# Moving a 2 KB load, six small operations and two weight loads in an attention and feed-forward kernel

## The reference

```python
def _rfs(xw, ab, AB, gs):
    dot_products = jnp.einsum('...d,rd->...r', xw, ab[:, None] * gs)
    correction = (0.5 * jnp.sum(xw * xw, axis=-1))[..., None] * (ab * ab)
    return 1.0 / math.sqrt(NUM_RFS) * AB * jnp.exp(dot_products - correction)
# ab = xis, AB = exp(xis)
weights = _rfs(input_weights, ab, AB, proj_matrix)
feats = _rfs(x, ab, AB, proj_matrix)
attn = einsum('bsr,or->bso', feats, weights)
x = layernorm(x + attn)
h = silu(x @ w_gate.T / 127) * (x @ w_up.T / 127)      # 3072 wide, int8 weights
x = layernorm(x + h @ w_down.T / 127)
```

## Time and profile before

| | |
|---|---|
| median of 3 runs | 740.23 us (739.68 to 740.56) |
| the profiled execution, its own time | 739.75 us |
| its span (slowest core, core 6) | 738.2 us |
| spans of the 8 cores | 735.7 to 738.2 us |
| TensorE matmul busy | 697.6 us, 95% |
| ScalarE busy | 197.1 us, 27% |
| VectorE busy | 183.9 us, 25% |
| mean granted TensorE clock, by core | 0.988 to 0.991 |

### The profile page before, as it was taken

The page is one execution under the profiler, slowest core; times in us unless marked ns, Lnnn a source line. Parts: engine busy times, 40 slices in busy tenths (PEclk is TensorE's granted clock), DMA queues, the critical chain, the costliest instruction groups (busy, mean ns, idle before and its releaser), DMA issues.

```text
span 738.2 us, 8975 instructions; the slowest of 8 cores (735.7 to 738.2 us)
## 1 busy us (share of the span) xinstructions
PE 697.6 (95%) x3357; PEld 314.1 (43%) x3424; DVE 183.9 (25%) x329; ACT 197.1 (27%) x322; POOL 9.1 (1%) x21
## 2 busy tenths in 40 slices
PE   2999999999959999999999999999999999999994
PEld 0333435343424444444444444444444444444442
DVE  1120335262532211121221122221222131211222
ACT  1223335252522111043311104231110523111122
POOL 2000000000000000000000000000000000000000
PEclk9999999999979999999999999999999999999998
DMA  8991030871084000001200000120000100000011
GB/s 120 168 353 44 1 57 1 211 303 57 2 334 179 0 1 1 1 28 58 87 0 1 1 1 29 58 86 1 0 1 1 57 29 29 0 1 2 1 58 57
DMA packets 5835, 44.63 MB, mean 60 GB/s; under 512 B 800, under 2 KB 800, under 8 KB 3104
## 3 DMA queue, kind: packets, MB, share of 16 engines
q0 software_dynamic: 2192, 27.27, 13.5%
q1 hardware_dynamic: 3600, 16.78, 6.0%
HBM read 30.42 MB, written 12.58 MB: 58 GB/s over the span
## 4 chain that ended last, share of the span: by engine, by line
PE 86%; DMA 7%; DVE 3%; issue 2%; ACT 1%; POOL 0%; DVEq 0%; ACTq 0%; SPq 0%; POOLq 0%
PE pt L624 23%; PE P L586 22%; PE P L682 22%; PE P L429 5%; DMA bfarena<-iwT 4%; PE P L276 4%; PE P L323 4%; DMA bfarena<-xfm 2%; PE pt L462 1%; PE P L688 1%; PE P L698 1%; PE P L435 1%; PE P L441 1%; PE P L281 1%; DVE bfarena L367 1%
## 5 line engine op out<-in xcount | busy, mean ns | idle before, releaser
L586 PE MATMUL P<-bfarena 128*128 128x512 bf16 x752 | 183.9, 383 | 0.9
L624 PE MATMUL pt<-bfarena 128*128 128x512 bf16 x753 | 180.3, 379 | 0.9
L682 PE MATMUL P<-bfarena 128*128 128x512 bf16 x721 | 162.2, 379 | 0.9
L637 DVE SCALAR_TENSOR_TENSOR bfarena<-pt,bfarena 128x512 bf16<-128x512 f32 x96 | 66.4, 692 | 245.2 <-PE pt L624 239.3
L605 ACT ACTIVATE bfarena<-P 128x512 bf16<-128x512 f32 x96 | 57.3, 597 | 239.6 <-PE P L586 235.6
L586 PEld LDWEIGHTS P<-bfarena 128*128 128x128 bf16 x768 | 75.4, 99 | 93.4 <-issue 3.5
L624 PEld LDWEIGHTS pt<-bfarena 128*128 128x128 bf16 x768 | 74.9, 98 | 92.4
L682 PEld LDWEIGHTS P<-bfarena 128*128 128x128 bf16 x736 | 71.9, 98 | 88.7
L367 DVE TENSOR_SCALAR_CACHE_REDUCE bfarena<-P 128x1024 bf16<-128x1024 f32 x32 | 39.2, 1225 | 199.0 <-PE P L698 145.3
L276 PE MATMUL P<-bfarena 128*128 128x512 bf16 x249 | 62.2, 388 | 2.8 <-DMA bfarena<-projT 2.5
L387 ACT ACTIVATE f32arena<-f32arena 128x1 f32<-128x1 f32 x32 | 9.4, 295 | 174.8 <-DVE f32arena L384 173.9
(11 more groups left out here) (54 smaller groups left out, 234.8 us busy)
## 6 DMA issues: line engine op xcount, KB each, us to landing
out<-f32arena SPq DMA_DIRECT2D x16, 512.0 KB, 2.7
bfarena<-wgT POOLq DMA_DIRECT2D x1, 6144.0 KB, 53.2
bfarena<-wdT POOLq DMA_DIRECT2D x3, 2048.0 KB, 14.7
bfarena<-wuT POOLq DMA_DIRECT2D x1, 4608.0 KB, 27.4
x1s<-bfarena SPq DMA_DIRECT2D x4, 1024.0 KB, 4.5
bfarena<-x1s SPq DMA_DIRECT2D x4, 1024.0 KB, 6.3
bfarena<-xfm POOLq DMA_DIRECT2D x3, 1024.0 KB, 15.1
bfarena<-projT POOLq DMA_DIRECT2D x2, 1024.0 KB, 18.6
```

Of the source, the lines that this page charges most:

```text
L586: return e.matmul(pg, bf(WGT_O + dk * 3072 + hc * 128, 128), bf(xb1 + dk * 512, 512), start=(dk == 0), stop=(dk == DK - 1))
L624: return e.matmul(puj, bf(wu_off + hc * 128, 128), bf(xb1 + dk * 512, 512), start=(dk == 0), stop=(dk == DK - 1))
L637: "vector", "VE", lambda e, j=j, hc=hc, puj=puj: e.scalar_tensor_tensor(hact_ap(hc, 0, 512), puj, 1.0 / 16129.0, sg_ap(j), OP.mult, OP.mult))
L682: e.matmul(P1[:, base + oh * 512:base + oh * 512 + 512], hact_ap(hc, m * 128, 128), bf(reg + (hc % 8) * 1024 + oh * 512, 512), start=(hc = ...
```

## The change

Four edits. (1) The load of xisr is issued after the two halves of the projection matrix instead of before them. (2) VectorE's six constant operations are emitted after the first tile's two squares instead of before them. (3) Of the three loads of wdT only the first is issued at the end of the first stage; the second is issued once gate block 2 is done and the third once gate block 4 is done. (4) The silu results go through two buffers instead of three, so silu j waits for product j-2.

```diff
@@ the arena's offsets
-SG3_O = WUT1_O + 18432
-BF_END = SG3_O + 512
+BF_END = WUT1_O + 18432
@@ the first loads
-        ev["ld_abrow"] = dma("gpsimd", "Lab", bfr(ABROW_O, 1024), xisr_h[:, :])
         ev["ld_projT"] = dma("gpsimd", "Lpj", bf(PROJT_O, 4096), projT_h[:, 0:4096])
         ev["ld_projT2"] = dma("gpsimd", "Lpj2", bf(PROJT_O + 4096, 4096),
                               projT_h[:, 4096:8192])
+        ev["ld_abrow"] = dma("gpsimd", "Lab", bfr(ABROW_O, 1024), xisr_h[:, :])
@@ the constants: these lines stood ahead of emit_ones_mm's definition
         emit_xsq(0)
+        ftmp = fa(FTMP_O, DK)
+        em.wait("vector", "XR", XR_ALL)
+        em.inc("vector", "VE", lambda e: e.memset(ones_col, 1.0))
+        em.inc("vector", "VE", lambda e: e.memset(epsc, 1e-5))
+        em.inc("vector", "VE", lambda e: e.memset(c512, 512.0))
+        em.inc("vector", "VE", lambda e: e.tensor_scalar_add(biasW, xisc, -LN32))
+        em.inc("vector", "VE", lambda e: e.tensor_mul(ftmp, xisc, xisc))
+        ev["ve_consts"] = em.inc("vector", "VE", lambda e: e.scalar_tensor_tensor(
+            biasF, ftmp, -512.0, biasW, OP.mult, OP.add))
+
         emit_ones_mm(0)
@@ the end of the first stage
         em.wait("gpsimd", "MM", ev["mm_z1", 4 * NT - 1])
-        for j, reg in enumerate(WDT_R):
-            ev["ld_wdT", j] = dma("gpsimd", "Lwd", bf(reg, 8192),
-                                  wdT_h[:, 8192 * j:8192 * (j + 1)])
+        ev["ld_wdT", 0] = dma("gpsimd", "Lwd", bf(WDT_R[0], 8192),
+                              wdT_h[:, 0:8192])
 
         def sg_ap(j):
-            k = j % 3
-            return bf(SG3_O, 512) if k == 2 else bf(SWROW_O + k * 512, 512)
+            return bf(SWROW_O + (j % 2) * 512, 512)
@@ emit_silu
-                if j >= 3:
-                    em.wait("scalar", "VE", ev["ve_h", j - 3])
+                if j >= 2:
+                    em.wait("scalar", "VE", ev["ve_h", j - 2])
@@ the first tile's loop of the second stage
                 for hc in range(4, HC):
+                    if hc in (6, 12):
+                        j = 1 if hc == 6 else 2
+                        em.wait("gpsimd", "MM", ev["mm_g", j * 2])
+                        ev["ld_wdT", j] = dma(
+                            "gpsimd", "Lwd", bf(WDT_R[j], 8192),
+                            wdT_h[:, 8192 * j:8192 * (j + 1)])
                     emit_gate(pi, hc)
                     emit_up(pi, hc)
```

More of the change, by code:

```diff
@@ L221, in emit_iwsq @@
                     bf(IWT_O + dk * 1024, 1024), OP.mult))
[L223 to L231, removed]
         def emit_ones_mm(t):
```

## The result

| | before | after |
|---|---|---|
| median of 8 runs each | 740.2 us | 746.46 us |
| ratio after to before | | 1.0089 (95% interval 1.0078 to 1.0100) |
| the profiled execution | 739.75 us | 746.69 us |
| its span (core 6 in both) | 738.2 us | 745.1 us |

What follows compares the result with a forecast made beforehand. TensorE, busy 95% of the span, was taken as the bound, so edits count only where it stands still or is made to. Terms 6.2 + 0 + 0 + 0 on 740.23 gave 746.4 us; 8-in-10 range 744.4 to 748.2.

Steps and rivals of the forecast that it cites:

- the mechanism: Start: xisr lands with the second projT half, so the first dot product waits until 25.6 us on core 6.
- two terms of the sum: First dot product on core 6: second projT half lands at 25.5 us, plus 0.1 us from landing to first matmul.
- The cover of 0.5 us: Ones-matmuls behind the first tile: core 6's stop for VectorE's last square swallows 0.5 of 6.7 us, leaving +6.2.
- each core's own length: First tile's dot products: each core keeps its earlier length, 18.91 us on core 6 and 20.11 on core 4.
- the bounds of 1.2 us: First tile: slow matmuls at TensorE's restart could shift the time by -1.2 to +1.2 us, giving 745.0 to 747.8.
- 2.6 us in the prediction: Start: part 2's cost if part 1's wait goes, 3.1 us later dot products less 0.5 us of cover.
- The chain's length: Start: second square, constants, eight ones-matmuls, table load; would allow core 6's dot products at 22.0 us, +3.1 us.
- rival (b): Start: row overtakes, eight ones-matmuls in one piece bring 2.4 GHz forward, halving the first block's 3.50 us; 741.2, chance 0.03.
- rival (a)'s overtaking: Start: the 2 KB row overtakes projT, then part 2's chain decides; +2.6 us, 742.8, chance 0.06.
- its 2 us of cover: First feed-forward tile: gate block 4 starts about 2 us after silu 2 frees its bank, so two buffers cost 0.
- the sum: Whole kernel: parts 1 to 4 cost 6.2 + 0 + 0 + 0 us, added to the 740.23 us median.

Runs made afterwards that it cites:

- three places in the queue: Row's load ahead of projT (kernel before), behind both projT halves (changed kernel, 746.46 us), or one load further back against the kernel before (753.39 us, ratio 1.0176).
- part 1 alone: Kernel before with only the 2 KB row's load moved behind both halves of projT: 746.31 against 740.33 us, ratio 1.0085.
- without part 1: Changed kernel with the row's load back ahead of projT, so parts 2, 3 and 4: 741.37 us against the kernel before at 740.12, ratio 1.0016.
- Another order at the change of stage: Kernel before with layer norm ends, then also gate and up blocks, reordered in three versions: 734.55, 735.17 and 733.94 us, ratios 0.9928, 0.9932 and 0.9915.

## Why the prediction was right

Forecast 746.4, measured 746.46; the mechanism was the one named, and no rival took place in the changed kernel.

- **Part 1.** The row's landing with the load ahead is shown by three places in the queue. The edit alone gives a ratio of 1.0085, all four together 1.0089. The first dot product was put at 25.6 on core 6 and came at 26.25: the projT half landed at about 25.8 instead of 25.5 in this execution, and 0.4 us lie between the row's landing and the first matmul, not the 0.1 read off projT's. These two terms of the sum were 0.6 us too small together. The cover of 0.5 us was used up as said: the 16 ones-matmuls ran unbroken in 3.65 us. On core 6 that is +7.3 at the dot products and +6.7 at line 323, where the prediction had 6.7 and 6.2.
- **The clock.** The first tile took 18.76 us on core 6 (26.25 to 45.01), 18.91 before. On the mean of the cores it was 19.5 against 19.4 us, although TensorE stood idle for 7 to 8 us instead of 2.5 to 4. With part 1 alone it was 19.5 behind 10 us. So the longer idle time changed nothing on the mean. Taking each core's own length is not shown to be right: it changed by -0.3 to +0.8 us from one profiled execution to the other (core 7: 19.17 to 19.93), which is inside the bounds of 1.2 us. The level in this stretch is read off the pace of the matmuls. The granted clock that the profile lists for core 6 before is 1.00 from 18 to 22 us, where eight matmuls take 3.50 us; in the changed kernel it is 0.50 from 24 to 28 us. So the mean granted clock, 0.984 to 0.991 after, reads lower than before without more slow matmuls in the first tile.
- **Part 2.** Hidden, as said: ScalarE's row was ready at 20.9, and TensorE waited 5 us longer. What it would cost uncovered was mis-sized: 2.6 us in the prediction, +1.2 us measured without part 1 and +0.5 to +0.8 alone. The chain's length was right (8.7 us from the second square to the first dot product, 8.8 in the prediction), but it was started from core 6, whose second group of ones-matmuls began at 14.57 us before, on the other cores at 13.04 to 14.10. On the mean of the cores the first dot product moved by 1.6 us, not 3.1. And part of the cores got 2.4 GHz earlier, which the prediction had only in rival (b). Rival (b)'s clock effect exists on some cores; rival (a)'s overtaking, on which it was hung, does not.
- **Part 3 and part 4.** 0 and 0, measured 0.9998 and 1.0000, with intervals of 0.0009 to 0.0010 to each side. For part 3 the wait of line 478 stayed (1.46 us against 1.54). Part 4 kept its 2 us of cover.
- **What the agreement hides.** The two profiled executions differ by 6.9 us, the medians by 6.3. So the last 0.6 us of the agreement is chance: the sum was good to about that. It was also luck that core 6 stood for the chip in both executions. After, it is not the latest at line 312 (core 3 is, at 51.66 us against 50.19), but its second gate block took 3.41 us and that of core 3 took 1.91, and so core 6 came last to the first up block (232.41 against 231.93).

Left open: why the eight ones-matmuls in one piece bring 2.4 GHz forward on some cores and not on others. The executions looked at give cases of each, and no kernel here separates the causes.

## What to carry to other kernels

A small load on a shared queue can cost nothing in bytes and much by its place, 2 KB and 6 us here: ask which engine waits for it, and put it ahead of the large loads that this engine can do without for longer. When a change moves several waits, work out each one's ready time and take the latest; the others are free only as long as that one stands, as part 2 shows. In a chain that crosses three engines, look at what stands in order on each: a layer norm's end that waits held up a copy that was ready. Another order at the change of stage was worth 5 to 6 us, about what the row's load had cost. When the time is that of the slowest core, look at all cores: a gain of 3.2 us on their mean at the end of a stage was 1.5 us in the time.

## What the runs showed of the hardware that was not expected

- A stop of 0.68 to 2.17 us between the first eight dot-product matmuls and the ninth was followed on four of eight cores by a second block wholly at 1.2 GHz (3.59 us against 1.92). On two of them, cores 0 and 4, the first block had already sped up (2.68 and 2.48 us), so the clock fell back. The length of the stop does not sort the cores: 0.68 us came before 3.59, 1.24 us (core 5) before 1.92. In the profiled executions of the kernel before, the changed kernel and each part alone, which have no such stop, no second block took more than 2.87 us. What sorts the cores stays open.
- Eight ones-matmuls in one piece (3.57 us), followed by 2.31 us of idle time, left some cores at 2.4 GHz for the next block (1.90 us) and others at 1.2 GHz (3.57 us) in the same execution.
- A store and a load of x1 that shared the engines with a wdT load took longer in the changed kernel: the store landed 9.9 us after its issue, 4.1 before, and the load of x1 for the next tile 8.3 us, 4.9 before. TensorE did not wait for either.
- At the change of stage the second gate block, behind an idle time of about 3 us, took 1.91 us on four cores and 2.8 to 3.3 on the other four in the same execution of the kernel before. That alone puts the cores up to 1.5 us apart.
